# A state-space layer with routed experts: which engine makes a state's term, and which takes a ReLU

## The reference

```
h = prelu(((gamma * (q k^T)) v) Wo + bo)                 # q, k, v from x
x_main, x_gate = split(h W_in + b_in)
xc = silu(x_main W_conv + b_conv)
B, C = split(xc W_bc + b_bc);  dt = softplus(xc W_dt + b_dt)
for each token t:  H = exp(dt * A) * H + dt * B[t] * xc[t];  y[t] = sum over 16 states (H * C[t])
h = layernorm(h + (y * silu(x_gate)) W_out + b_out)
f = relu(h Wi + bi)
for two layers:    f = relu(shared(f) + expert[route](f) + f)
h = layernorm(h + f Wo + bo)
```

## Time and profile before

| | us |
|---|---|
| median of three runs | 353.38 |
| the profiled execution's own time | 353.91 |
| its span in the profile | 352.1 |
| TensorE busy (matrix products) | 284.7 |
| VectorE busy | 266.4 |
| GpSimd busy | 257.5 |
| ScalarE busy | 182.1 |
| GpSimd's 64 products hc | 153.7 |
| GpSimd's 41 products ub | 96.8 |

### The profile page before, as it was taken

One profiled execution on the slowest core, in us unless ns is written; L12 is line 12 of the kernel. 1 busy time (PEld: TensorE's weight loads), 2 busy tenths in 40 slices (PEclk: granted clock), 3 DMA queues, 4 the chain that ended last, 5 costly groups with the idle time before them and its releaser, 6 DMA issues.

```text
span 352.1 us, 4445 instructions
## 1 busy us (share of the span) xinstructions
PE 284.7 (81%) x1406; PEld 164.7 (47%) x1406; DVE 266.4 (76%) x288; ACT 182.1 (52%) x251; POOL 257.5 (73%) x113
## 2 busy tenths in 40 slices
PE   8998838784975899998995999978656595798895
PEld 4423302332443343475732434767454275776483
DVE  2566669988788999987989899879798958973130
ACT  3005823247885344789564347893665564432403
POOL 0027067998999999999999799999979986973000
PEclk9999959997689899999899899985859857579998
DMA  7960595866699997777899876679999765783001
GB/s 246 419 244 0 176 313 212 247 260 253 208 320 301 293 400 251 259 241 226 311 339 310 294 262 218 238 262 300 314 321 336 297 248 208 264 252 82 1 2 30
DMA packets 43000, 85.88 MB, mean 244 GB/s; under 512 B 7904, under 2 KB 24800, under 8 KB 42720
## 3 DMA queue, kind: packets, MB, share of 16 engines
q1 hardware_dynamic: 42576, 84.43, 71.2%
q10 hardware_dynamic: 400, 1.17, 1.2%
HBM read 75.62 MB, written 1.57 MB: 219 GB/s over the span
## 4 chain that ended last, share of the span: by engine, by line
PE 22%; DVE 13%; issue 8%; ACT 7%; POOL 5%; DMA 4%; SPq 1%; DVEq 0%; POOLq 0%; ACTq 0%
DVE h L1026 6%; PE tail L633 5%; PE acc_y L558 4%; DMA c_row<-bc_dram 4%; DVE decay L1007 3%; POOL hc L907 3%; POOL ub L898 2%; PE work L504 2%; PE acc_r L515 2%; PE tail L618 2%; ACT decay_own L708 2%; PE tail L614 1%; PE decay L438 1%; SPq L377 1%; PE work L633 1%
## 5 line engine op out<-in xcount | busy, mean ns | idle before, releaser
L907 POOL TENSOR_TENSOR hc<-h,c_row 128x1024 f32<-128x1024 f32 x64 | 153.7, 2402 | 27.9 <-DVE h L1026 26.4
L898 POOL TENSOR_TENSOR ub<-u,b_row 128x1024 f32<-128x1024 f32 x41 | 96.8, 2361 | 11.6 <-DVE u L1064 11.2
L708 ACT ACTIVATE decay<-delta,neg_a 128x512 f32<-128x512 f32 (+1 forms) x64 | 51.3, 812 | 78.8 <-DVE h L1026 78.7
L558 PEld LDWEIGHTS acc_y<-pack,hc 128*128 128x128 f32 x512 | 66.4, 159 | 44.2 <-issue 27.7
L558 PE MATMUL acc_y<-pack,hc 128*128 128x128 f32 x512 | 79.7, 306 | 4.7 <-POOL hc L907 4.7
L1026 DVE TENSOR_TENSOR_SCAN h<-decay,ub 128x512 f32<-128x512 f32 (+1 forms) x41 | 66.0, 1611 | 14.6 <-POOL ub L898 7.5
L504 PE MATMUL work<-q,kT 64*128 64x512 f32 x112 | 34.8, 699 | 18.1 <-DVE mixed L1044 13.8
L1044 DVE TENSOR_TENSOR mixed<-gam,work 128x512 f32<-128x512 f32 x56 | 35.5, 676 | 7.8 <-PE work L504 7.1
L730 ACT ACTIVATE decay<-u 128x512 f32<-128x512 f32 (+1 forms) x42 | 26.2, 640 | 21.7 <-DVE h L1026 21.5
L515 PE MATMUL acc_r<-mixed,v_sb 128*64 128x512 f32 x128 | 36.5, 650 | 1.1 <-DVE mixed L1044 1.0
L1007 DVE TENSOR_TENSOR decay<-decay,b_row 128x512 f32<-128x512 f32 (+1 forms) x40 | 30.6, 764 | 8.0 <-ACT decay L730 6.7
(11 more groups left out here) (149 smaller groups left out, 301.3 us busy)
## 6 DMA issues: line engine op xcount, KB each, us to landing
b_row<-bc_dram SPq DMA_DIRECT2D x64, 512.0 KB, 4.9
c_row<-bc_dram SPq DMA_DIRECT2D x64, 512.0 KB, 5.1
group_w<-expert_w SPq DMA_DIRECT2D x64, 128.0 KB, 4.7
gam<-gammaT SPq DMA_DIRECT2D x8, 512.0 KB, 10.3
expert_w<-routed_w SPq DMA_DIRECT2D x1, 2048.0 KB, 18.3
x_in<-xT SPq DMA_DIRECT2D x4, 256.0 KB, 8.7
out<-res SPq DMA_DIRECT2D x8, 128.0 KB, 3.5
pack<-packed ACTq DMA_DIRECT2D x1, 788.0 KB, 7.0
```

The lines of the kernel that those rows point to most:

```text
L558: mm = nc.tensor.matmul(acc_y[:, c * P:(c + 1) * P], hc[:, k % 3, c * P:(c + 1) * P], ident, start=(n == 0 and c % 4 == 0), stop=(n == STA ...
L708: op = nc.scalar.activation(target[:, columns], delta[:, b % 2, columns], ACT.Exp, scale=neg_a[:, n:n + 1])
L898: nc.gpsimd.tensor_tensor(ub[:, j % 3, :], u[:, b % 2, :], b_row[:, k % 3, :], ALU.mult)\
L907: nc.gpsimd.tensor_tensor(hc[:, k % 3, :], h[:, k % 3, :], c_row[:, k % 3, :], ALU.mult)\
```

## The change

Image 0's list of states whose term VectorE makes goes from 0, 4, 8, 10, 14 to 0, 3, 6, 8, 10, 12, 14. So states 3, 6 and 12 change to VectorE and state 4 changes to GpSimd. For all images, the ReLUs behind the second expert layer (both halves, `USE_L2` and `USE_L2 + 1`) move from VectorE, where they stood at the end of steps 12 and 13, to ScalarE, in the same steps. The other images' lists stay as they were.

```
--- before.py
+++ after.py
@@ -39,7 +39,7 @@
 
 
 VECTOR_STATES = [STATES * b + s for b in range(IMAGES)
-                 for s in ((0, 4, 8, 10, 14) if b < IMAGES - 1 else range(0, STATES, 2))]
+                 for s in ((0, 3, 6, 8, 10, 12, 14), (0, 4, 8, 10, 14), (0, 4, 8, 10, 14), range(0, STATES, 2))[b]]
 GPSIMD_STATES = [k for k in range(STATES * IMAGES) if k not in VECTOR_STATES]
 
 
@@ -66,9 +66,9 @@
     (14, LATE): ((USE_OUT2, REST),), (15, LATE): ((USE_VAR2, WHOLE),), (17, EARLY): ((USE_ROWS, WHOLE),),
 }
 
-ACT_TAIL = {4: USE_OUT1, 5: USE_VAR1, 6: USE_F0, 7: USE_F0 + 1, 14: USE_OUT2, 15: USE_VAR2, 17: USE_ROWS}
-
-DVE_TAIL = {2: USE_YT, 3: USE_YT + 1, 6: USE_VAR1, 8: USE_L1, 11: USE_L1 + 1, 12: USE_L2, 13: USE_L2 + 1, 16: USE_VAR2}
+ACT_TAIL = {4: USE_OUT1, 5: USE_VAR1, 6: USE_F0, 7: USE_F0 + 1, 12: USE_L2, 13: USE_L2 + 1, 14: USE_OUT2, 15: USE_VAR2, 17: USE_ROWS}
+
+DVE_TAIL = {2: USE_YT, 3: USE_YT + 1, 6: USE_VAR1, 8: USE_L1, 11: USE_L1 + 1, 16: USE_VAR2}
 
 TAIL_FROM = {
     USE_OUT1: (USE_YT, USE_YT + 1), USE_L1: (USE_F0,), USE_L1 + 1: (USE_F0 + 1,), USE_L2: (USE_L1,),
@@ -829,6 +829,11 @@
                     nc.scalar.activation(res[:, :], bank[:, :], ACT.Copy).then_inc(rows_ready, 1)
                     act.wait_ge(rows_ready, b + 1)
                     act.sem_inc(tail_taken(b, use)[0], 1)
+                if use in (USE_L2, USE_L2 + 1):
+                    i = use - USE_L2
+                    act.wait_ge(*tail_filled(b, use))
+                    nc.scalar.activation(f[:, i * HALF:(i + 1) * HALF], bank[:, :], ACT.Relu)\
+                        .then_inc(tail_taken(b, use)[0], 1)
                 if use in (USE_F0, USE_F0 + 1):
                     i = use - USE_F0
                     act.wait_ge(*tail_filled(b, use))
@@ -1076,7 +1081,7 @@
                     dve.wait_ge(read, before + 2)
                     nc.vector.tensor_tensor(yg[:, at], gate[:, b % 2, at], bank[:, :], ALU.mult)\
                         .then_inc(tail_taken(b, use)[0], 1)
-                if use in (USE_L1, USE_L1 + 1, USE_L2, USE_L2 + 1):
+                if use in (USE_L1, USE_L1 + 1):
                     i = (use - USE_L1) % 2
                     dve.wait_ge(*tail_filled(b, use))
                     nc.vector.tensor_scalar(f[:, i * HALF:(i + 1) * HALF], bank[:, :], 0.0, None, ALU.max)\
```

## The result

The changed kernel takes 358.98 us (median of 4 runs, 356.65 to 360.17) against 352.54 us of the kernel before in the same set. The ratio is 1.0146 with a 95% interval of 1.0088 to 1.0203, which is 5.1 us more (3.1 to 7.2). The forecast was slower, 356.5 us in a range of 351.5 to 359.8. Its direction and its places held; the size of one place did not.

A forecast was written before the change was run, and what follows sets the result against it. VectorE's own-product steps were taken to bound image 0, TensorE and ScalarE the last stretch. +2.2 + 2.1 - 0.75 - 0.4 = +3.15 us on 353.91, 357.06, less 0.53 to the median: 356.5 us, range 351.5 to 359.8.

The forecast's parts named there:

- States 3 and 6, +0.5: Image 0, first half: GpSimd's relief arrives in front of a VectorE that is late itself; +0.5 us.
- State 12, +1.7: Image 0: ScalarE makes decay_own before the copies of u, so VectorE's scans come later; 2.2 us with the 0.5 included.
- The bounds: Image 0's whole term of 2.2 us: between 0.5 us and 3.1 us, the latter with the late row.
- SyncE's later loads: Image 0: b_row for state 15 and the loads behind it shift; priced at nothing, up to 0.5 us if late.
- ReLUs in image 1, +2.1: End of image 1: ReLUs queue behind ScalarE's side evictions, residual 2.8 us later, image 2's first product 2.1 us later.
- The order of the file: Sign in image 1: K0 eviction, ReLU, second fill, V eviction, ReLU in single file.
- rival (c): TensorE's clock falls in image 1 through new waits, slowing second fill and V projection: +5.0, 358.4 us; chance 0.15.
- Returns, -0.75 and -0.4: ReLUs on ScalarE, no projections following: image 2 gains 0.75 us, image 3 0.4 us because TensorE's fills hold the end.
- the forecast's sign of under 1: Image 3: last scans about 2 us closer to their image's start while ln_q moves by under 1 us.
- Rival (a): Image 0: GpSimd sets the pace, so two products less give -4.7 us; -5.9 in all, 347.5 us; chance 0.10.
- the forecast's own range: Whole kernel: 354.5 to 358.5 us, chance 0.50, half of it taken to lie beyond the 356.9 that makes 1%.

The follow-up runs named there:

- the version that beats both: Old states, second-layer ReLUs of all images on ScalarE ahead of the side evictions, against the kernel before: ratios 0.9891 and 0.9900 in two sets.
- the three state lists: Kernel before with only image 0's list changed: the whole new list 1.0089, state 12 alone 1.0029, states 3 and 6 in place of 4 1.0040.

## Why the prediction was right, and where it was not

*States 3 and 6, +0.5.* Right: VectorE's step with its own product is the longer one, and state 7 came some 0.4 us later. GpSimd idled 1.5 us before two of its products.

*State 12, +1.7.* Right in cause and size. decay_own goes first, VectorE waits 2.2 to 2.5 us for the copy, and the scans behind it shift by 1.66 us alone and 2.4 with states 3 and 6. The bounds hold the 1.5 of the changed kernel's profile too. SyncE's later loads cost nothing that shows.

*ReLUs in image 1, +2.1.* This is the term that was mis-sized. The order of the file was right row by row. At full clock it cost 1.0 us and not 2.1, since K0's projection ran at full speed (1.12 us) where the execution of the earlier trace rows did it in 2.06 us, in its low stretch, and the file starts at K0. The profile with unused products and the old states fits: K0's projection took 1.62 us there, and the file cost 1.7. In the changed kernel's execution it cost 7.0 us: from state 12's +2.1 to +9.1 at image 2's first scan. The 6 us between are the clock's, which was rival (c), at 0.15; the profiles of the ReLUs alone and of the unused products, with the same file at a clock of 1.00, show 1.0 in their place. I had priced it at 1.9 us, taking only the second fill and V's projection at the lower pace. The low clock lasted from the fill to the residual and beyond, and every piece in the file paid, with ScalarE's and VectorE's waits in between: slower pieces stretched the file. That TensorE's idling brings the fall is shown as far as filling the waits ends it; what decides in which execution it comes stays open. All four runs of the changed kernel were above 356.6 us. The Trainium skill, "TensorE: Matmul & The Clock Gate", What's actually happening, says that the throttled state is the default and activity releases it; the traces agree in part: 0.57 where TensorE idled and 1.00 when unused products filled the same waits, but 1.00 as well behind the same waits in the profile of the ReLUs alone. With seven of ten runs slow when only the ReLUs moved, the chance of (c) should have been well over one half.

*Returns, -0.75 and -0.4.* Right as far as these profiles tell. Image 2's is 0.2 to 1.0 us. In image 3 VectorE and GpSimd gain 1.78 us, and the span behind the last scan's start grows from 37.04 to 38.48 us, so 0.34 is left, because TensorE's fills, and not VectorE, set ln_q. Measured from image 3's first scan ln_q comes 1.1 us earlier, just over the forecast's sign of under 1, with 0.89 of it ahead of state 13. These figures hang on the clock of these executions. With a second fill of 2.61 us (the second profile of the version that beats both) the span behind the last scan is 36.8 us and the gain stays whole; and with the ReLUs on VectorE and a second fill of 1.90 us (states 3 and 6 alone) the last scan is 7.49 us behind that of state 13, with no ReLU moved.

The sum was 3.15 us; with the measured terms of the profiled execution it is -0.56 (start) + 1.47 (image 0) + 0.60 (image 1, step 3) + 6.98 - 1.76 - 2.67 (image 3 to the last scan) + 1.44 (behind it) = 5.50 us, which is 357.6 - 352.1. The 0.60 of image 1 is not the change's: that step is 0.3 to 1.4 us longer than in the profile shown of before in all other profiles but one. The 2.67 has 0.89 in it that lies ahead of state 13, and two profiles of one and the same kernel, the version that beats both, differ by 2.95 us from image 3's first scan to its last. The measured time lay in the stated range partly by luck: the sum missed by 2.4 us, and the range reached that far up only for rival (c). Without the fall's 5.9 us the same terms leave -0.4 us, and the changed kernel with its waits filled is 0.8 us slower (-0.4 to 1.9), which includes none. So it is the fall, and not the sum's terms, that made the change clearly slower.

Rival (a), GpSimd's relief, is refuted by the three state lists, none of them faster. In the chances one step was loose: 356.9 to 358.5 is two fifths of the forecast's own range, and not half.

## What to carry to other kernels

Taking a product off the busiest-looking engine pays only in steps that wait for it: count, for each kind of step, the time on both engines before choosing how many to move. When an eviction moves to another engine, read what stands ahead of it in that engine's queue and whether TensorE's next two pieces wait on both; here, with the old states, the same ReLUs on the same engine made the kernel 1.0% faster one place earlier, and 2.4 us slower in the median one place later. A new wait on TensorE like these (1.2 us) in a stretch that is bound by it should be priced twice: with the clock as it was, and with all the work behind it at half clock.

## What the runs showed of the hardware that I had not expected

The clock's fall is not the same in each execution of one kernel. With only the ReLUs moved, ten runs of the same program gave 351 us three times and 356 to 359 seven times, and four unused products in TensorE's waits left one group at 350 to 356. Two traces of one kernel show such a difference directly. In those of the version that beats both, the granted clock from image 3's first scan to its last is 0.70 and 0.83, the same stretch takes 62.20 and 59.25 us, and the second fill of its tail 3.51 and 2.61. A term of under a microsecond that is read from one profile of each kernel needs a second pair.

A product of VectorE from two SBUF tensors meets GpSimd: in both kernels the three hc products that run beside u (one at each head that is made during a scan) take 3.25 us and not 2.36 (3.26 at 105.77 in the changed kernel, u at 105.61), and none that runs beside a product in PSUM does.
